# An attention probability split by one affine select on GpSimd instead of two products, the low weight halves of wo all on GpSimd, and a difference of values on VectorE

## The chip, the cores and the metric
The kernel runs on one core of one Trainium2 chip. The metric is device time in microseconds of one launch. Before the change the median of three runs is 810.45 us (809.56 to 811.89).

## The reference, cut to what matters
Three blocks work on x (4 sequences of 256 tokens, 512 channels): a feed-forward block with a router and low-rank experts, attention, and the feed-forward block again. The change lies in the attention, which has 32 query heads in 8 groups of 4 (one key/value head each) and a sliding window of 128:

```python
q = _rope((x @ wq).reshape(B, S, 32, 128), pos)
k = _rope((x @ wk).reshape(B, S, 8, 128), pos)
v = (x @ wv).reshape(B, S, 8, 128)
allowed = (j <= i) & (j > i - 128)
attn = softmax(where(allowed, q @ k.T * sm_scale, neg))
out = (attn @ v).reshape(B, S, 4096) @ wo
```

All is float32. A query of the second 128 tokens of a sequence sees keys of the first block with j > i - 128 and keys of the second block with j <= i. Within 128 columns these two sets don't overlap and fill the row, so one 128 x 128 tile P holds all its probabilities: column c stands for key c of block 1 where c <= row, and for key c of block 0 elsewhere.

## The kernel before, in words
Every float32 product is made of three passes in a shorter format: each operand is split in a high half (a rounded copy, made by ScalarE) and a low half (operand minus high half, made by VectorE or GpSimd), and TensorE computes high x high, high x low and low x high.

The attention runs over 8 groups g (the first and the last are written out, the six between are a loop), each with two halves hf (two sequences each, 512 tokens), each with 8 slots s. A slot is one head of one sequence; u counts all 128. TensorE's queue in a slot is, in this order: in slot 0 first the transposes of the values (`v_transpose`), then 9 of the 72 matmuls that project the next half's k, q0 to q3 and v (`project`, L1106), the scores of the next head (L1125 to L1128), the two transposes of the previous head's probabilities (`p_transpose`, L1136), and, for four heads at once, `values` (L1149, in slots 1 and 5) and `out_project` (L1165, in slots 2, 3, 6, 7). An `m` names the six projected tiles, 0 for k, 1 to 4 for q, 5 for v. Tiles 0 to 5 end in slots 1, 2, 3, 5, 6 and 7 of a half. They alternate between two PSUM banks A[0] and A[1]; the first matmul of a tile waits (`a_free`) until the tile two before has been read by `rope_cos`, or, for v, by `v_lo`.

Rope of a tile: ScalarE swaps its halves (`rope_swap`, L528), GpSimd multiplies them by the sine (`rope_sin`, L370), VectorE multiplies by the cosine (`rope_cos`, L782) and adds (`rope_sum`, L791), ScalarE makes the high half (L536), GpSimd the low half (`rope_lo`, L387).

Softmax of a head: VectorE adds masks and takes minima (`softmax_min`, L804 to L812; L812 merges the two key blocks of the second queries in one 128 x 128 tile), ScalarE exponentiates (L554), VectorE takes the reciprocal of the sum and multiplies twice (`softmax_norm`, L817 and L820), TensorE transposes, ScalarE copies the high half (`p_hi`, L562), VectorE makes the low half (`p_lo`, L826). Then GpSimd parts the tile of the second queries (`p_part`, L377): it waits for `p_lo` and multiplies both halves by a table with ones where the column is causal (to block 2 of pT) and by the complement (in place, block 1). `values` computes, for the second queries, block 1 x v0 + block 2 x v1, and waits (`parted`) ahead of these six matmuls.

Order on VectorE in a slot: `v_lo` in slot 0, an addition of the attention's output to x (L839), `softmax_norm`, in slot 5 of half 0 `wo_split`, `rope_sum`, `rope_cos`, `p_lo`, `softmax_min` of the next head, `o_lo` (L832) in slots 1 and 5. On GpSimd: `rope_sin`, `p_part`, `rope_lo`, `weights`.

Weights come by DMA in pieces of 128 x 512 through a ring of five buffers (`raw`); ScalarE makes the high halves (L500), and SyncE's queue starts the next piece when the low half of the one before in the same buffer is done. The low halves of wk, wq and wv are made on GpSimd (`split_lo`, L362). Of wo's four pieces the first two are made there in slot 4 of half 0, the other two on VectorE (`wo_split`, L861) in slot 5. The second pass of `out_project`, in slot 6, waits for all four.

Of the kernel before, what the change touches and what calls it, by code (L numbers as in the profile page):

```python
# [24 lines left out]
P = 128  # L25
# [50 lines left out]
def macaron(nc, x_in, wq, wk, wv, wo, w_base, b_base, w_router, lora_a, lora_b, ident_in, mask_in, side_in, rope_in, out):  # L76
    ctx = ExitStack()
    with ctx:
# [11 lines left out]
        side = sb("side", [P, 2, P])  # L90
# [96 lines left out]
        conv_hi, conv_lo, wo_lo = sem("w_hi_done"), sem("w_lo_done"), sem("wo_lo_done")  # L187
        a_done, a_free = sem("proj_done"), sem("proj_bank_read")
        vcopy_done, vt_done = sem("vT_copied"), sem("v_transposed")
# [5 lines left out]
        parted = sem("pT_parted")  # L195
# [8 lines left out]


# [14 lines left out]
        WO_POOL = G // 2  # L220

        def wk_lo(g):
            return 8 * g + 1

        def wq_lo(g, i):
            return 8 * g + 2 + i

        def wv_lo(g):
            return 8 * g + 6

        def wo_lo_pool(g, i):
            return 8 * g + 7 + i

        def wo_lo_dve(g, i):
            return 2 * g + 1 + i - WO_POOL

# [20 lines left out]
        def _(sp):  # L257
# [8 lines left out]
            sp.dma_start(side[:, :, :], side_in).then_inc(tables_landed, 16)  # L266
# [13 lines left out]
            def group(g, last):  # L280
                order = [("o", i) for i in range(G)]
                if not last:
                    order += [("k", 0)] + [("q", i) for i in range(KT)] + [("v", 0)]
                for kind, i in order:
                    if kind == "k":
                        sp.wait_ge(conv_lo, wv_lo(g))
                        off, src = 4, wk_src(wk, g + 1)
                    elif kind == "o":
                        sp.wait_ge(conv_lo, wq_lo(g, i))
                        off, src = i, wo[bass.ds(g * (G * DH) + i * DH, DH), :]  # L290
                    elif kind == "q":
                        if i < WO_POOL:
                            sp.wait_ge(conv_lo, wo_lo_pool(g, i))
                        else:
                            sp.wait_ge(wo_lo, wo_lo_dve(g, i))
# [34 lines left out]
        def _(pool):  # L330
            nc.gpsimd.memset(ones, 1.0).then_inc(preset, 1)
            nc.gpsimd.memset(ebuf[:, :, :, :], -1.0).then_inc(preset, 1)
            nc.gpsimd.memset(two[:, :, :], -1.0).then_inc(preset, 1)

# [37 lines left out]
            def p_part(u, s):  # L372

                pool.wait_ge(ptlo_done, u + 1)
                both, h = pT_both[:, :, 1, s % G, :], s % G
                for blk in (2, 1):
                    last = nc.gpsimd.tensor_tensor(pT_both[:, :, blk, h, :], both.bitcast(F32),  # L377
                                                   side[:, blk - 1, :].unsqueeze(1).broadcast_to([P, 2, P]), ALU.mult)
                last.then_inc(parted, 1)
# [9 lines left out]
            def weights(g, hf, s, last):  # L389
                if hf == 0 and s == 4:  # L390
                    for i in range(WO_POOL):
                        split_lo(wo_pos(g, i), (6 + i) % RING, wo_s[0][:, i, :], wo_s[1][:, i, :])
# [48 lines left out]
        def _(act):  # L441
# [96 lines left out]
            def v_copy(j):  # L538

                act.wait_ge(a_done, 6 * j + 6)  # L540
                act.wait_ge(sum_done, 5 * j + 4)
                nc.scalar.activation(swap[:, 1, :], A[1][:, :], ACT.Copy).then_inc(vcopy_done, 1)
# [119 lines left out]
        def _(dve):  # L662
# [130 lines left out]

            def v_lo(j, par):
                dve.wait_ge(vhi_done, j + 1)
                nc.vector.tensor_tensor(v[1][:, par, :, :], A[1][:, :].rearrange("p (t n) -> p t n", t=HT),
                                        v[0][:, par, :, :].bitcast(F32), ALU.subtract).then_inc(a_free, 1)
# [59 lines left out]
            def wo_split(g):  # L857

                for i in range(WO_POOL, G):
                    dve.wait_ge(conv_hi, wo_pos(g, i) + 1)  # L860
                    nc.vector.tensor_tensor(wo_s[1][:, i, :], raw[:, (6 + i) % RING, :], wo_s[0][:, i, :].bitcast(F32),  # L861
                                            ALU.subtract).then_inc(wo_lo, 1)

            def group(g, first, last):
                for hf in range(2):
                    for s in range(SLOTS):
# [10 lines left out]
                        if hf == 0 and s == 5:  # L877
                            wo_split(g)
# [4 lines left out]
                        if not (start and s == 0):  # L883
                            p_lo(u - 1, s - 1)
                        if s == 0 and last and hf == 1:
# [62 lines left out]
            dve.wait_ge(tables_landed, 48)  # L948
# [20 lines left out]
            rope_sum(0, 4)  # L969
            softmax_min(0, 0)  # L970
# [35 lines left out]
        def _(pe):  # L1006
# [104 lines left out]
            def v_transpose(j):  # L1111

                pe.wait_ge(vcopy_done, j + 1)
# [25 lines left out]
            def values(beta, par, b, j):  # L1139
# [4 lines left out]
                for i, blocks in enumerate((((0, 0),), ((1, 0), (2, 1)))):  # L1144
                    if i:
                        pe.wait_ge(parted, 4 * beta + 4)
                    todo = [(blk, kb, a, c) for blk, kb in blocks for a, c in PASSES]
                    for n, (blk, kb, a, c) in enumerate(todo):
                        last = mm(O[i][:, :], v[a][:, par, 2 * b + kb, :], pT[c][:, blk, :, :],  # L1149
# [3 lines left out]
            def out_project(beta, par, i, g):  # L1153
# [4 lines left out]
                for n, (a, c) in enumerate(((0, 0), (0, 1), (1, 0))):  # L1158
                    if c:
                        pe.wait_ge(conv_lo, wo_lo_pool(g, WO_POOL - 1))  # L1160
                        pe.wait_ge(wo_lo, wo_lo_dve(g, G - 1))
# [146 lines left out]
```

## Time and profile before
| | |
|---|---|
| median of 3 runs | 810.45 us |
| profiled execution, span from first to last instruction | 807.1 us |
| TensorE matmul busy | 739.6 us, 92% |
| VectorE busy | 677.0 us, 84% |
| GpSimd busy | 508.7 us, 63% |
| ScalarE busy | 417.0 us, 52% |
| granted TensorE clock, mean | 0.979 |

An engine's busy time in this profile holds the time in which one of its instructions has started and can't go on, so an instruction's duration can be longer than its work. PE is TensorE, DVE VectorE, ACT ScalarE, POOL GpSimd.

### The profile page before, as it was taken

How to read it: one execution, taken by the hardware profiler on the slowest of the kernel's cores; microseconds unless marked ns; L12 is line 12 of the kernel's file. 1: busy time of each engine (PE TensorE's matmuls, PEld its weight loads, DVE VectorE, ACT ScalarE, POOL GpSimd, SP SyncE). 2: the span in 40 equal slices, each digit the busy share in tenths (PEclk: the TensorE clock that was granted, in tenths of full speed). 3: DMA queues.
4: the chain of work that ended last, by engine and by line, in shares of the span. 5: the costliest groups of instructions: out<-in, count | busy, mean ns of one | idle time of the engine just before them, and what ended most of it. 6: DMA issues, size and time to landing. Idle time of an engine off the chain costs nothing.

```text
span 807.1 us, 14015 instructions
## 1 busy us (share of the span) xinstructions
PE 739.6 (92%) x3692; PEld 611.2 (76%) x3692; DVE 677.0 (84%) x2060; ACT 417.0 (52%) x1122; POOL 508.7 (63%) x578
## 2 busy tenths in 40 slices
PE   5989778999899989998999899999899899988998
PEld 3878557878777878787878777877788787876876
DVE  3888878988898888889888888888978898888795
ACT  2324474556655665555555555565557545654321
POOL 0384387766777667757775776577667776664720
PEclk8899999999999999999999999999999999999999
DMA  9040002100120011001100120002100210020002
GB/s 293 1 170 14 1 4 84 45 1 2 66 66 1 0 65 52 13 0 65 52 13 0 52 65 13 0 20 71 39 0 0 70 47 0 2 105 0 2 27 79
DMA packets 25986, 32.25 MB, mean 40 GB/s; under 512 B 5849, under 2 KB 14425, under 8 KB 25442
## 3 DMA queue, kind: packets, MB, share of 16 engines
q1 hardware_dynamic: 21216, 30.56, 11.5%
q10 hardware_dynamic: 4738, 1.31, 0.7%
q8 instruction: 14, 0.23, 0.1%
q14 instruction: 18, 0.15, 0.1%
HBM read 27.67 MB, written 4.19 MB: 39 GB/s over the span
## 4 chain that ended last, share of the span: by engine, by line
PE 51%; DVE 28%; issue 11%; ACT 5%; ACTq 2%; POOL 2%; DVEq 1%
PE bank L1106 17%; PE bank L1165 16%; DVE sm L812 4%; PE bank L1128 4%; PE bank L1149 4%; PE bank L1072 4%; DVE rot L791 3%; ACT prob L554 3%; DVE rot L782 2%; DVE wo_lo L861 2%; PE bank L1136 2%; DVE sm L805 2%; DVE prob L820 2%; DVE pT_hi_lo L826 2%; DVE oT_lo L832 2%
## 5 line engine op out<-in xcount | busy, mean ns | idle before, releaser
L377 POOL TENSOR_TENSOR pT_hi_lo<-pT_hi_lo,side 128x256 fp32r<-128x256 f32 x256 | 186.9, 751 | 118.6 <-DVE pT_hi_lo L826 118.6
L554 ACT ACTIVATE prob<-sm,nmax 128x128 f32<-128x128 f32 x256 | 101.0, 395 | 204.9 <-DVE sm L812 204.9
L370 POOL TENSOR_TENSOR swap<-swap,rope 128x512 f32<-128x512 f32 x80 | 105.8, 1322 | 95.5 <-ACT swap L528 95.5
L820 DVE TENSOR_SCALAR prob<-prob,rinv 128x128 f32<-128x128 f32 x256 | 123.9, 525 | 4.5
L528 ACT ACTIVATE swap<-bank 64x512 f32<-64x512 f32 x160 | 94.9, 593 | 11.3 <-PE bank L1106 8.7
L387 POOL TENSOR_TENSOR q_lo<-rot,q_hi 128x512 fp32r<-128x512 f32 x64 | 84.5, 1321 | 6.8 <-ACT q_hi L536 6.8
L1165 PE MATMUL bank<-wo_hi,oT_hi 128*128 128x512 f32 x256 | 79.4, 434 | 0.3 <-DVE x L839 0.3
L812 DVE TENSOR_TENSOR sm<-sm 128x128 f32<-128x128 f32 x128 | 79.3, 619 | 0.0
L1106 PE MATMUL bank<-xnT_hi,wq_hi 128*128 128x512 f32 x256 | 72.3, 395 | 6.5 <-DVE rot L782 5.3
L1106 PE MATMUL bank<-xnT_lo,wq_hi 128*128 128x512 f32 x256 | 73.4, 390 | 0.0
L1106 PE MATMUL bank<-xnT_hi,wq_lo 128*128 128x512 f32 x256 | 72.6, 396 | 0.9 <-POOL wq_lo L362 0.9
L562 ACT ACTIVATE pT_hi_lo<-bank 128x256 fp32r<-128x256 f32 x128 | 48.9, 382 | 46.4 <-PE bank L1136 38.3
L1165 PE MATMUL bank<-wo_lo,oT_hi 128*128 128x512 f32 x256 | 70.1, 396 | 0.0
L1165 PE MATMUL bank<-wo_hi,oT_lo 128*128 128x512 f32 x256 | 68.7, 390 | 0.0
L1149 PE MATMUL bank<-pT_hi_lo,v_hi 128*128 128x512 f32 x192 | 63.6, 412 | 1.7 <-POOL pT_hi_lo L377 0.9
L791 DVE TENSOR_TENSOR rot<-rot,swap 128x512 f32<-128x512 f32 x80 | 64.2, 803 | 0.0
L1106 PEld LDWEIGHTS bank<-xnT_hi,wq_hi 128*128 128x128 f32 x256 | 47.3, 188 | 20.0 <-DVE rot L782 8.7
L782 DVE TENSOR_TENSOR rot<-bank,rope 128x512 f32<-128x512 f32 x80 | 54.7, 684 | 9.0 <-ACT swap L528 9.0
L1136 PE MATMUL bank<-ident,prob 128*128 128x128 f32 x256 | 50.7, 281 | 10.7 <-DVE pT_hi_lo L826 10.7
L826 DVE TENSOR_TENSOR pT_hi_lo<-bank,pT_hi_lo 128x256 fp32r<-128x256 f32 x128 | 53.3, 416 | 8.2 <-ACT pT_hi_lo L562 6.9
L536 ACT ACTIVATE q_hi<-rot 128x512 fp32r<-128x512 f32 x64 | 40.2, 629 | 37.3 <-DVE rot L791 37.2
L1128 PE MATMUL bank<-k_hi_lo,q_hi 128*128 128x256 f32 x256 | 59.2, 314 | 0.0
(148 smaller groups left out, 1705.6 us busy)
## 6 DMA issues: line engine op xcount, KB each, us to landing
raw<-in_L_attn_wq SPq DMA_DIRECT2D x32, 256.0 KB, 2.9
raw<-in_L_attn_wo SPq DMA_DIRECT2D x32, 256.0 KB, 2.7
x<-in_L_attn_x SPq DMA_DIRECT2D x4, 512.0 KB, 7.8
raw<-in_L_attn_wk SPq DMA_DIRECT2D x8, 256.0 KB, 2.5
raw<-in_L_attn_wv SPq DMA_DIRECT2D x8, 256.0 KB, 2.6
out<-x SPq DMA_DIRECT2D x8, 256.0 KB, 2.0
raw<-in_L_ffn_W_base ACTq DMA_DIRECT2D x4, 256.0 KB, 5.3
wb_keep_hi<-q_hi SPq DMA_DIRECT2D x1, 1024.0 KB, 4.8
```

The lines of the kernel that those rows point to most:

```text
L370: nc.gpsimd.tensor_tensor(w, w, tab, ALU.mult).then_inc(t2_done, 1)
L377: last = nc.gpsimd.tensor_tensor(pT_both[:, :, blk, h, :], both.bitcast(F32), side[:, blk - 1, :].unsqueeze(1).broadcast_to([P, 2, P]), AL ...
L387: nc.gpsimd.tensor_tensor(lo, rot[:, m % 2, :], hi.bitcast(F32), ALU.subtract).then_inc(qlo_done, 1)
L528: last = nc.scalar.activation(swap[a:a + half, m % 2, :], A[m % 2][b:b + half, :], ACT.Copy)
L554: last = nc.scalar.activation(prob[:, s % 2, lo:hi], sm[:, s % 2, lo:hi], ACT.Exp, bias=nmax[:, s % 2, i:i + 1], scale=-1.0, accum_out=rsu ...
L791: nc.vector.tensor_tensor(rot[:, m % 2, :], rot[:, m % 2, :], swap[:, m % 2, :], ALU.add).then_inc(sum_done, 1)
L812: nc.vector.tensor_tensor(sm[:, s % 2, P:2 * P], sm[:, s % 2, P:2 * P], sm[:, s % 2, 2 * P:3 * P], ALU.min).then_inc(min_done, 1)
L820: last = nc.vector.tensor_scalar(prob[:, s % 2, lo:hi], prob[:, s % 2, lo:hi], rinv[:, s % 2, i:i + 1], None, ALU.mult)
L1106: last = mm(A[m % 2][:, :], w, xnT[b][:, d, hf * HALF:(hf + 1) * HALF], start=(i == 0), stop=(i == 11))
L1128: last = mm(S[s % 2][:, 2 * P:4 * P], q[a][:, hf, h, q1], k[c][:, hf, b * SEQ:(b + 1) * SEQ], start=(n == 0), stop=(n == 2))
L1149: last = mm(O[i][:, :], v[a][:, par, 2 * b + kb, :], pT[c][:, blk, :, :], start=(n == 0), stop=(n == len(todo) - 1))
L1165: last = mm(C[:, :], oT[a][:, par, i, h, :], wo_s[c][:, h, :], start=(h == 0 and n == 0), stop=(h == G - 1 and n == 2))
```

## The change
The values of the second key block are replaced by the difference v1 - v0: ScalarE copies only v0 of the transposed values to SBUF (two of the four 128-column blocks of A[1]), and a new VectorE instruction per half, `v_diff`, subtracts that copy from v1; `v_transpose` waits for it. Block 1 of pT then stays the whole P and is not written by `p_part`; block 2 is P where causal, zero elsewhere, by one affine select, so that P v0 + causal(P)(v1 - v0) equals the sum before. The number of matmuls stays. The wait for `parted` moves three matmuls later. The table `side` and its DMA go. All four low halves of wo are made on GpSimd in slot 4 of half 0, `wo_split` goes, and SyncE's waits follow.

```diff
             def p_part(u, s):
                 pool.wait_ge(ptlo_done, u + 1)
-                both, h = pT_both[:, :, 1, s % G, :], s % G
-                for blk in (2, 1):
-                    last = nc.gpsimd.tensor_tensor(pT_both[:, :, blk, h, :], both.bitcast(F32),
-                                                   side[:, blk - 1, :].unsqueeze(1).broadcast_to([P, 2, P]), ALU.mult)
-                last.then_inc(parted, 1)
+                pool.sem_inc(mask_turn, 1)
+                h = s % G
+                nc.gpsimd.affine_select(pT_both[:, :, 2, h, :], pT_both[:, :, 1, h, :].bitcast(F32),
+                                        pattern=[[0, 2], [1, P]], compare_op=ALU.is_ge, fill=zero,
+                                        base=0, channel_multiplier=-1).then_inc(parted, 1)
...
             def weights(g, hf, s, last):
                 if hf == 0 and s == 4:
-                    for i in range(WO_POOL):
+                    for i in range(G):
                         split_lo(wo_pos(g, i), (6 + i) % RING, wo_s[0][:, i, :], wo_s[1][:, i, :])
...
-                nc.scalar.activation(swap[:, 1, :], A[1][:, :], ACT.Copy).then_inc(vcopy_done, 1)
+                nc.scalar.activation(v_half(swap[:, 1, :], 0), v_half(A[1][:, :], 0), ACT.Copy).then_inc(vcopy_done, 1)
...
+            def v_diff(j):
+                dve.wait_ge(vcopy_done, j + 1)
+                nc.vector.tensor_tensor(v_half(swap[:, 1, :], 1), v_half(A[1][:, :], 1), v_half(swap[:, 1, :], 0),
+                                        ALU.subtract).then_inc(vdiff_done, 1)
...
-                        if hf == 0 and s == 5:
-                            wo_split(g)
...
                             p_lo(u - 1, s - 1)
+                        if m == 5:
+                            v_diff(2 * g + hf + 1)
...
-                    if i:
-                        pe.wait_ge(parted, 4 * beta + 4)
                     todo = [(blk, kb, a, c) for blk, kb in blocks for a, c in PASSES]
                     for n, (blk, kb, a, c) in enumerate(todo):
+                        if n == len(PASSES):
+                            pe.wait_ge(parted, 4 * beta + 4)
```

## Rows read from the trace of the kernel before

**Rows 1.** The page: busy time, share, instructions; then shares of the last-ended chain.
```profile
PE 739.6 (92%) x3692; PEld 611.2 (76%) x3692; DVE 677.0 (84%) x2060; ACT 417.0 (52%) x1122; POOL 508.7 (63%) x578
...
PE 51%; DVE 28%; issue 11%; ACT 5%; ACTq 2%; POOL 2%; DVEq 1%
```
**Rows 2.** TensorE's waits: total us, times, longest us.
```profile
PE bank L1106 <- DVE rot L782: 30.1, 17, 3.7
PE bank L1136 <- DVE pT_hi_lo L826: 10.7, 12, 1.7
```
**Rows 3.** Groups: busy us, mean ns of one, idle before and its releaser.
```profile
L1106 PE MATMUL bank<-xnT_hi,wv_hi 128*128 128x512 f32 x64 | 23.1, 448 | 25.2 <-DVE rot L782 24.8
```
**Rows 4.** Stretches: length, busy PE, PEld, DVE, ACT, POOL, PEclk, DMA share, GB/s.
```profile
388.57:473.17 84.60, 79.88 (x397) 66.48 (x396) 72.46 (x216) 48.88 (x133) 58.91 (x61) 0.98 0.10 31
...
125.00:128.40 3.40, 3.40 (x13) 2.96 (x12) 3.37 (x11) 2.27 (x7) 2.33 (x4) 0.50 0.16 57
208.60:212.00 3.40, 3.40 (x18) 2.95 (x19) 3.32 (x12) 1.44 (x5) 2.74 (x3) 1.00 0.41 146
...
715.50:718.90 3.40, 3.40 (x13) 2.97 (x12) 3.32 (x12) 2.15 (x7) 1.04 (x3) 0.50 0.22 39
```
**Rows 5.** Timeline of VectorE from 452.8 us: start, length, instruction, count.
```profile
452.83 0.42 DVE L826 TENSOR_TENSOR pT_hi_lo<-bank,pT_hi_lo 128x256 fp32r<-128x256 f32 x1 [0.52 <-ACT pT_hi_lo L562]
...
454.05 0.87 DVE L812 TENSOR_TENSOR sm<-sm 128x128 f32<-128x128 f32 x1
455.87 0.17 DVE L817 RECIPROCAL rinv<-rsum 128x2 f32<-128x2 f32 x1 [0.95 <-ACT prob L554]
456.07 2.58 DVE L820 TENSOR_SCALAR prob<-prob,rinv 128x128 f32<-128x128 f32 x2
458.57 2.37 DVE L861 TENSOR_TENSOR wo_lo<-raw,wo_hi 128x512 fp32r<-128x512 f32 x2
460.87 0.68 DVE L782 TENSOR_TENSOR rot<-bank,rope 128x512 f32<-128x512 f32 x1
```
**Rows 6.** Timeline of GpSimd over the same stretch.
```profile
453.34 1.43 POOL L377 TENSOR_TENSOR pT_hi_lo<-pT_hi_lo,side 128x256 fp32r<-128x256 f32 x2 [1.90 <-DVE pT_hi_lo L826]
454.73 1.33 POOL L387 TENSOR_TENSOR q_lo<-rot,q_hi 128x512 fp32r<-128x512 f32 x1
456.01 2.56 POOL L362 TENSOR_TENSOR wo_lo<-raw,wo_hi 128x512 fp32r<-128x512 f32 x2
458.51 1.28 POOL L370 TENSOR_TENSOR swap<-swap,rope 128x512 f32<-128x512 f32 x1
```
**Rows 7.** Timeline of TensorE: the stall of slot 5/6 and what follows it.
```profile
457.59 1.07 PE L1106 MATMUL bank<-xnT_hi,wq_lo 128*128 128x512 f32 x4
461.60 0.96 PE L1106 MATMUL bank<-xnT_hi,wv_hi 128*128 128x512 f32 x3 [2.94 <-DVE rot L782]
```
**Rows 8.** Lines L812 and L820: ns min/median/max of one, first and last start.
```profile
L812 DVE TENSOR_TENSOR sm<-sm x128: 285/856/1381, 94.1 to 755.7; 128x128 f32<-128x128 f32 x128
...
L820 DVE TENSOR_SCALAR prob<-prob,rinv x256: 272/286/1339, 97.7 to 757.6; 128x128 f32<-128x128 f32 x128
```
**Rows 9.** Groups: the removed, moved and nearest operations.
```profile
L377 POOL TENSOR_TENSOR pT_hi_lo<-pT_hi_lo,side 128x256 fp32r<-128x256 f32 x256 | 186.9, 751 | 118.6 <-DVE pT_hi_lo L826 118.6
L362 POOL TENSOR_TENSOR wo_lo<-raw,wo_hi 128x512 fp32r<-128x512 f32 x16 | 20.3, 1293 | 0.0
L826 DVE TENSOR_TENSOR pT_hi_lo<-bank,pT_hi_lo 128x256 fp32r<-128x256 f32 x128 | 53.3, 416 | 8.2 <-ACT pT_hi_lo L562 6.9
L249 POOL TENSOR_TENSOR nt<-nt,var 128x2 f32<-128x2 f32 x12 | 2.5, 205 | 0.9
```
**Rows 10.** Timeline of GpSimd at the start: its cheapest instruction of such width.
```profile
0.88 0.14 POOL L332 MEMSET ebuf<- 128x64 f32 x1
```
**Rows 11.** Timelines around a transpose of values: VectorE's low half, then TensorE.
```profile
428.41 0.41 DVE L826 TENSOR_TENSOR pT_hi_lo<-bank,pT_hi_lo 128x256 fp32r<-128x256 f32 x1
...
429.98 0.60 PE L1115 MATMUL bank<-ident,swap 128*128 128x128 f32 x4
```
**Rows 12.** Timeline of VectorE in slot 1 of half 1, behind two wq pieces.
```profile
480.33 2.57 DVE L820 TENSOR_SCALAR prob<-prob,rinv 128x128 f32<-128x128 f32 x2
```

More of the change, by code:

```diff
@@ L89, in macaron @@
         mask = sb("mask", [P, 3 * P])
-        side = sb("side", [P, 2, P])
         rope = sb("rope", [P, 4, SEQ])
@@ L186, in macaron @@
         raw_landed = [sem(f"raw_landed{i}") for i in range(RING)]
-        conv_hi, conv_lo, wo_lo = sem("w_hi_done"), sem("w_lo_done"), sem("wo_lo_done")
+        conv_hi, conv_lo = sem("w_hi_done"), sem("w_lo_done")
         a_done, a_free = sem("proj_done"), sem("proj_bank_read")
-        vcopy_done, vt_done = sem("vT_copied"), sem("v_transposed")
+        vcopy_done, vdiff_done, vt_done = sem("vT_copied"), sem("vT_diff"), sem("v_transposed")
         swap_done, t2_done, sum_done = sem("swap_done"), sem("sin_done"), sem("rope_sum_done")
@@ L194, in macaron @@
         rinv_done, norm_done = sem("rinv_done"), sem("norm_done")
-        parted = sem("pT_parted")
+        parted, mask_turn = sem("pT_parted"), sem("mask_turn")
         t_done, pthi_done, ptlo_done = sem("pT_done"), sem("pT_hi"), sem("pT_lo")
@@ L203, in wait, with v_half @@
                 eng.wait_ge(s, n)
+        def v_half(t, i):
+            return t.rearrange("p (b i n) -> p b i n", b=2, i=2)[:, :, i, :]
         def wk_pos(g):
@@ L216, in wo_pos, with wo_lo @@
             return 10 * g + 6 + i
-        WO_POOL = G // 2
         def wk_lo(g):
-            return 8 * g + 1
+            return 10 * g + 1
         def wq_lo(g, i):
-            return 8 * g + 2 + i
+            return 10 * g + 2 + i
         def wv_lo(g):
[L229 to L235, printed above, removed]
+            return 10 * g + 6
+        def wo_lo(g, i):
+            return 10 * g + 7 + i
         def rstd_steps(engine, then, t0, t1):
@@ L265, in _ @@
             sp.dma_start(mask[:, :], mask_in).then_inc(tables_landed, 16)
-            sp.dma_start(side[:, :, :], side_in).then_inc(tables_landed, 16)
             sp.dma_start(rope[:, :, :], rope_in).then_inc(tables_landed, 16)
@@ L291, in group @@
                     elif kind == "q":
[L292 to L295, printed above, removed]
+                        sp.wait_ge(conv_lo, wo_lo(g, i))
                         off, src = 5 + i, wq_src(g + 1, i)
@@ L333, in _ @@
             nc.gpsimd.memset(two[:, :, :], -1.0).then_inc(preset, 1)
+            zero = nc.gpsimd.to_reg(0.0)
             def bias(f, t):
@@ L855, in ffn_start @@
                     x_lo(2, 1)
[L857 to L862, printed above, removed]
             def group(g, first, last):
@@ L946, in _ @@
             ffn_out(0, NT // 2 - 1)
-            dve.wait_ge(tables_landed, 48)
+            dve.wait_ge(tables_landed, 32)
             rope_cos(0, 0)
@@ L969, in _ @@
             rope_sum(0, 4)
+            v_diff(0)
             softmax_min(0, 0)
@@ L1111, in v_transpose @@
             def v_transpose(j):
-                pe.wait_ge(vcopy_done, j + 1)
+                pe.wait_ge(vdiff_done, j + 1)
                 for t in range(HT):
@@ L1159, in out_project @@
                     if c:
-                        pe.wait_ge(conv_lo, wo_lo_pool(g, WO_POOL - 1))
-                        pe.wait_ge(wo_lo, wo_lo_dve(g, G - 1))
+                        pe.wait_ge(conv_lo, wo_lo(g, G - 1))
                     if a:
```

## The prediction
> **What bounds the kernel now.** I read the page first. TensorE is busy 92% of the span, and the chain that ended last is 51% TensorE and 28% VectorE [rows 1]: neither engine bounds it alone, so the question is where TensorE stands still and for whom. The list of waits answers: 30.1 us for the cosine product of rope (L782) and 10.7 us for the low half of the probabilities (L826), both VectorE's [rows 2]. Of the 30.1, the grouped lines give 24.8 to one place, the first matmul of a v tile [rows 3], once in each of 8 groups, 3.1 us each. Next the clock: a group takes 84.6 us at a mean of 0.98 [rows 4]. Right behind this stall the granted clock is 0.50, the lower level of 1.2 GHz, over 3.4 us in six of the eight groups, the first and last of which are shown, and 1.00 (2.4 GHz) behind the one of 208.6 and behind one more [rows 4]. At half clock 3.4 us hold 1.7 us of work, so the stall is followed by another 6 x 1.7 = 10 us of loss.
>
> Then I asked why VectorE is late there. L820 is 0.29 us in the median and up to 1.34; L812 is 0.29 at the least and 0.86 in the median [rows 8]. The long ones lie beside GpSimd. In one place two L820 take 2.58 us from 456.07 to 458.65 while GpSimd runs the two wo pieces from 456.01 to 458.57; the two of `wo_split` then take 2.37 with `rope_sin` beside them [rows 5, 6]. So a VectorE instruction with all its operands in SBUF waits until the running GpSimd instruction ends, gets in between two of them, and meets the next. L782 and L826, which read PSUM, don't wait. L812 shows the commonest case: `p_lo` ends at 453.25, GpSimd's first product starts at 453.34 and its second some 0.71 later; L812 starts at 454.05, 0.80 behind `p_lo` and just behind the start of the second product, and is held until that ends, 0.58 us lost [rows 5, 6]. More than half of the 128 heads show it, by the median.
>
> **Part 1, wo.** VectorE loses two L861 between L820 and the cosine product, 2.37 us [rows 5]. GpSimd gains two L362, 2 x 1.29 = 2.6 us, in slot 4 [rows 9]. I walk through the stall: with all else as before, L820 still ends at 458.65, held by the first two wo pieces; the cosine product starts there instead of at 460.87, and TensorE, free from 458.66, goes on about 0.6 us later instead of 2.94 [rows 5, 7]. That is 2.3 us per group. GpSimd's pieces three and four end at about 461.2, `rope_sin` of this slot at 462.5. They now hold L812 of slot 5 (near 460.4, to 461.2) and one of slot 6's two L820 under the wk piece, but all that stands over 1 us ahead of its old time. The second pass of `out_project` needs the fourth piece: TensorE is there near 461.9. SyncE's next wq pieces start with the same pieces at nearly the same time and have slot 6 to land.
>
> **Part 2, the select.** 256 products of 0.751 us go, 128 selects come [rows 9]. The trace has no select. From below: no input at all, a memset of 64 columns, is 0.14 us [rows 10]. From above: as slow as the two products, 1.50; nothing excludes more (a rival). I take the nearest row, one product of the same 128 x 256: 0.75 us. Then GpSimd is free, or at a boundary, at 0.09 + 0.05 (the added semaphore instruction, an estimate of mine) + 0.75 = 0.89 behind `p_lo`, L812 arrives at 0.80 and is held 0.1 instead of 0.6. Everything queued behind the product, `rope_lo` and the weight pieces, starts 0.65 earlier, and so L820 is held less: behind the two wq pieces it is 2.57 for two [rows 12]. With wo's part, L820 of slot 5 meets two wo pieces 0.6 us earlier, so that the cosine product ends near 458.7, when TensorE arrives: the stall goes but for 0.5 on average, 2.6 x 8 = 21 us. The clock had no stall of 3 us to fall after: 10 us. The other waits on VectorE, 30.1 - 24.8 + 10.7 = 16.0 [rows 2, 3], lie in half 1 at the end of a VectorE chain of four or five slots; saving about 0.5 per L812 and 0.6 at the L820s there is near 2 us per group, as much as the stalls. Some will be taken by what is late next, TensorE's wait for its own order or ScalarE's copy (8.2 us of idle at L826 already [rows 9]); I take 9 of the 16.
>
> The Trainium skill has a rule that would change this term. By it (GPSIMD Engine Reference, section 7, Performance pitfalls for Q7 kernels) a loop body that compares and selects runs at 1.03 to 2.03 cycles per element; with 256 elements at the 1.2 GHz of section 1 that is an estimate of 0.22 to 0.43 us of loop. No run here shows it; the products' 0.751 is the nearest that the trace has. By the rule the select would end before L812 arrives, which is the first rival below.
>
> **Part 3, v_diff.** 16 new VectorE instructions of 128 x 256 from PSUM: 0.416 by L826 [rows 9], 0.33 apart. They read PSUM and one SBUF tile like L826, so GpSimd doesn't hold them. ScalarE's copy halves in width. `p_lo` of slot 7 ends at 428.82; the difference ends near 429.2, and TensorE transposes at 429.98 [rows 11]: hidden by `out_project`, 0.8 us to spare; without that cover it would be 0.4 x 16 = 6.6. It does push `softmax_min` and so L812 and ScalarE's exponential back 0.33, 16 times, 5.3 us at most, and at least nothing, where TensorE is the later of the two. With the longer holds that wo's pieces make in slots 5 and 6 I charge 5 us in all. Ahead of the first group nothing covers VectorE's wait for ScalarE's copy: 1 us.
>
> **Part 4, the rest.** The wait for `parted` moved behind three matmuls and the table's DMA at the start cost nothing and gain under 1 us: TensorE's wait there is hidden in the 16.
>
> **Sum** against the profiled execution: 807.1 - 21 - 10 - 9 + 5 + 1 = 773.1 us. The run around it is 810.45 - 807.1 = 3.35 more (the median against this one execution): **776 us**. For this case alone, 764 to 788.
>
> **Rivals.**
> 1. *The select is fast, below 0.65 us.* Then the next GpSimd instruction (1.29 to 1.33 us, [rows 6, 9]) starts before L812 and holds it to 0.14 + D + 1.29, at D = 0.5 to 1.93 behind `p_lo`, against 1.52 now: 0.4 later wherever something is queued. L820 then finds GpSimd free more often. For it: a small two-input product costs 0.205, so the fixed part is small [rows 9]. Against: two-input products cost 0.751, and the select has to form its condition for each element. Price: the 9 us of part 2 are not gained and the stall of slot 5 keeps 0.2 more: 776 + 9 + 2 = 787.
> 2. *The select is as slow as both products, 1.2 to 1.6.* Only part 1 is left: 2.3 x 8 = 18, the clock's 10, less 5 + 1: 810.45 - 22 = 788.
> 3. *The select is slower than 1.7, and VectorE is held by it at L812 in nearly every slot.* L812 then waits D - 0.66 instead of 0.58, and all GpSimd work behind it is later. The gain of 22 us over some 110 heads is 0.2 each, so it decides from D = 1.5 + 0.2 = 1.7. At D = 2.0 it is 0.5 x 110 = 55 us: 810 + 55 - 22 = 843, slower. For it: no row bounds the select from above. Against: it reads one tensor, not two, and each product takes 0.75.
> 4. *The burst of four wo pieces moves the stall instead of taking it away*: L812 and L820 of slots 5 and 6 held by up to 2.6 us, as GpSimd works in its own order, and the next wait stands at slot 6 or 7. Gain of the v tile's stall halved and the clock's kept to half: 810 - 10 - 5 - 9 + 6 = 792.
>
> **How the numbers follow.** Forecast 48%, rival 1 16%, rival 2 11%, rival 3 12%, rival 4 13%. The predicted time is 776. The low end of the range is the forecast's own with all 16 us and no new cost, 810.45 - 21 - 10 - 16 = 763, taken down to 760; the high end takes in rivals 1, 2 and 4 with a few us, 805. Rival 3 is outside. Within 0.3% of 810.45 (808 to 813, about what a measurement can tell from no change) lie the seams between rivals 2, 4 and 3: 4%. Faster 84%, slower 12%.
>
> **What would show it.** The select's mean duration, 0.75, decides most: under 0.65 rival 1, over 1.7 rival 3. L812's median falls from 0.86 to about 0.4. The idle before the v tile's first matmul falls from 25.2 us to about 4, and no stretch at 0.50 follows it. A group takes near 80 us. L1115 doesn't wait for the new difference. GpSimd's busy time falls by 187 - 96 - 21 = 70 us. I am wrong if VectorE's chain still ends later than TensorE's queue in slot 5 though `wo_split` is gone.

## The result and the profile after

The changed kernel takes 777.57 us (median of 4 runs, 777.01 to 778.18) against 810.51 before: ratio 0.9591, 95% interval 0.9577 to 0.9606, so 33 us or 4.1% faster. The prediction was 776 with 760 to 805, and 84% on faster. Time and direction came out; several of the terms that make up the 776 did not, and their errors cancelled. That is what the experiments are about. The ratios below are to runs of the kernel before taken beside each kernel, whose medians lie from 809.9 to 811.2 us.

The page of the kernel after, against [rows 1]: busy times, then the shares of the chain that ended last.

```profile
PE 731.0 (94%) x3692; PEld 606.8 (78%) x3692; DVE 643.7 (83%) x2060; ACT 411.2 (53%) x1122; POOL 392.9 (51%) x466
...
PE 47%; DVE 31%; issue 10%; ACT 9%; ACTq 2%; DVEq 1%; POOL 0%
```

GpSimd lost 116 us of work, VectorE 33, and yet VectorE's share of the chain rose from 28% to 31%. TensorE's waits, as in [rows 2], and the one place of [rows 3]:

```profile
PE bank L1101 <- DVE rot L777: 13.3, 13, 2.2
...
PE bank L1131 <- DVE pT_hi_lo L827: 4.8, 4, 2.2
PE bank L1159 <- DVE x L840: 4.6, 8, 0.7
```
```profile
L1101 PE MATMUL bank<-xnT_hi,wv_hi 128*128 128x512 f32 x64 | 22.4, 436 | 12.1 <-DVE rot L777 12.1
```

The stall at the v tile fell from 25.2 to 12.1 us, the transposes' from 10.7 to 4.8; a new one of 4.6 stands at `out_project`, for the addition to x that frees its bank. The stretches, columns as in [rows 4]: one group, the 3.4 us behind the first v stall, and behind a later one.

```profile
375.90:456.30 80.40, 78.26 (x398) 65.37 (x397) 68.17 (x217) 48.17 (x133) 44.51 (x47) 1.00 0.11 33
124.20:127.60 3.40, 3.40 (x13) 2.91 (x13) 3.32 (x13) 1.74 (x6) 3.10 (x4) 0.50 0.51 165
446.00:449.40 3.40, 3.40 (x19) 2.89 (x19) 3.32 (x12) 1.96 (x6) 2.91 (x3) 1.00 0.51 151
```

A group takes 80.4 us in place of 84.6. Between 95 and 735 us the clock stood at its lower level twice for 3.4 us, before six times, and TensorE's gaps sum to 25.2 us where they were 44.5.

What such a stretch costs can be read inside one trace, because some groups have one and others, behind the same stall, have none. Here is a group of each kind in the kernel before (from one transpose to the same one of the next group), then in e2, the kernel after without its wo edit, where a stall of 2.5 us is left:

```profile
187.82:271.89 84.07, 78.80 (x399) 65.08 (x398) 72.36 (x217) 48.85 (x134) 58.90 (x61) 1.00 0.10 32
356.27:440.84 84.57, 79.85 (x398) 66.58 (x397) 72.44 (x217) 48.86 (x134) 58.91 (x61) 0.98 0.09 31
```
```profile
349.59:431.41 81.82, 79.27 (x398) 66.54 (x397) 69.62 (x219) 48.06 (x134) 41.88 (x44) 0.98 0.10 32
431.41:513.28 81.87, 78.22 (x399) 65.36 (x397) 69.63 (x219) 48.06 (x134) 41.89 (x44) 1.00 0.11 32
```

With the stretch TensorE is busy 1.05 us longer. Yet the group takes only 0.3 to 0.5 us longer before (84.4 to 84.6 against 84.1) and no longer in e2: at least half of it falls in time in which TensorE would have waited. Between groups without such a stretch the change is worth 84.1 - 80.4 = 3.7 us, 8 times, some 30 of the 33 us.

The new select and the two VectorE operations beside GpSimd, grouped (mean ns of one is the second number behind the bar), against [rows 9] and, for the next two, one line's minimum, median and maximum against [rows 8]:

```profile
L372 POOL TENSOR_SCALAR_AFFINE_SELECT pT_hi_lo<-pT_hi_lo 128x256 fp32r<-128x256 f32 x128 | 52.8, 413 | 145.8 <-DVE pT_hi_lo L827 145.0
```
```profile
L813 DVE TENSOR_TENSOR sm<-sm x128: 285/1185/1301, 96.0 to 725.6; 128x128 f32<-128x128 f32 x128
```
```profile
L821 DVE TENSOR_SCALAR prob<-prob,rinv x256: 272/285/1343, 98.5 to 727.3; 128x128 f32<-128x128 f32 x128
```

The select is 0.41 us, not 0.75. L813, the merge that was L812, did not get shorter: its median rose from 0.86 to 1.19. The timelines show why, first VectorE, then GpSimd, in slot 4:

```profile
438.69 0.42 DVE L827 TENSOR_TENSOR pT_hi_lo<-bank,pT_hi_lo 128x256 fp32r<-128x256 f32 x1
...
439.90 1.20 DVE L813 TENSOR_TENSOR sm<-sm 128x128 f32<-128x128 f32 x1
442.06 0.17 DVE L818 RECIPROCAL rinv<-rsum 128x2 f32<-128x2 f32 x1 [0.95 <-ACT prob L549]
442.26 2.57 DVE L821 TENSOR_SCALAR prob<-prob,rinv 128x128 f32<-128x128 f32 x2
444.75 0.68 DVE L777 TENSOR_TENSOR rot<-bank,rope 128x512 f32<-128x512 f32 x1
```
```profile
439.28 0.41 POOL L372 TENSOR_SCALAR_AFFINE_SELECT pT_hi_lo<-pT_hi_lo 128x256 fp32r<-128x256 f32 x1 [3.00 <-DVE pT_hi_lo L827]
439.66 1.30 POOL L382 TENSOR_TENSOR q_lo<-rot,q_hi 128x512 fp32r<-128x512 f32 x1
440.91 5.07 POOL L357 TENSOR_TENSOR wo_lo<-raw,wo_hi 128x512 fp32r<-128x512 f32 x4
445.92 1.30 POOL L365 TENSOR_TENSOR swap<-swap,rope 128x512 f32<-128x512 f32 x1
```

The select is over at 439.69, the low half of rope starts at 439.66, and L813, at 439.90, is held by that until 441.0. Two L821 still take 2.57 us beside the first two of the four wo pieces, and the cosine product L777 starts at 444.75 directly behind them; before, `wo_split` stood between.

**A measure for the holds.** For each kernel I took the VectorE instructions behind 95 us whose operands all lie in SBUF (the merge of the minima, the two products of the normalization, the rope sum, `wo_split`) and summed by how much each record is longer than a free one (0.288, 0.286, 0.684, 0.680), shorter ones counted as nothing. Before it is 119.8 us (merge 41, normalization 62, rope sum 8, wo 9), after 92.5 (75, 17, 0, none). This sum, TensorE's gaps and the count of stretches at half clock, the last two between 95 and 735 us, stand beside each run below. Ahead of 95 us, where the kernels do the same, the clock was at half for 10.2 to 17.1 us in one profiled execution and another, so a few us between two executions need not be the change's.

| kernel | median us | ratio to before, interval | holds us | gaps us | half clock |
|---|---|---|---|---|---|
| before | 810.5 | 1 | 119.8 | 44.5 | 6 |
| after | 777.6 | 0.9591, 0.9577 to 0.9606 | 92.5 | 25.2 | 2 |
| e1 wo's part only | 803.8 | 0.991, 0.9891 to 0.9928 | 126.1 | 43.0 | 1 |
| e2 select's part only | 789.6 | 0.975, 0.9726 to 0.9775 | 93.9 | 32.5 | 5 |
| e3 one product | 782.8 | 0.9659, 0.9635 to 0.9683 | 84.2 | 27.2 | 4 |
| e4 low half first | 768.9 | 0.9483, 0.9466 to 0.9499 | 73.8 | 22.8 | 3 |
| e5 yield | 761.7 | 0.9416, 0.9376 to 0.9457 | 59.2 | 20.3 | 0 |
| e6 one select for four | 781.2 | 0.9641, 0.9616 to 0.9666 | 87.3 | 26.6 | 5 |
| e7 no difference | 778.4 | 0.9601, 0.9583 to 0.9619 | 98.5 | 28.9 | 0 |
| e8 e4, wk later | 753.3 | 0.9288, 0.9270 to 0.9306 | 63.9 | 13.8 | 0 |
| e9 e5, wk later | 767.7 | 0.9472, 0.9449 to 0.9494 | 66.5 | 23.4 | 0 |
| e11 e3, yield | 767.8 | 0.9477, 0.9454 to 0.9500 | 63.5 | 22.2 | 0 |
| e12 e1, wk later | 810.2 | 1.0003, 0.9991 to 1.0015 | 133.9 | 44.8 | 3 |
| e13 products, order of e8 | 814.4 | 1.0053, 1.0036 to 1.0071 | 130.9 | 45.5 | 3 |

### The profile page after: what moved, and what is told of

Its sections match the earlier page's. It is cut to its first block, busy times and chain, and to the rows that moved or that the text cites. A ratio compares the mean times of both kernels' runs of the same rounds, so it can differ in the third digit from the quotient of the medians.

```text
span 776.5 us, 13949 instructions
## 1 busy us (share of the span) xinstructions
PE 731.0 (94%) x3692; PEld 606.8 (78%) x3692; DVE 643.7 (83%) x2060; ACT 411.2 (53%) x1122; POOL 392.9 (51%) x466
## 4 chain that ended last, share of the span: by engine, by line
PE 47%; DVE 31%; issue 10%; ACT 9%; ACTq 2%; DVEq 1%; POOL 0%
PE bank L1101 16%; PE bank L1159 12%; DVE sm L813 7%; PE bank L1144 5%; PE bank L1067 4%; ACT prob L549 4%; PE bank L1123 3%; DVE sm L806 3%; DVE rot L777 3%; DVE oT_lo L833 2%; DVE rot L786 2%; DVE pT_hi_lo L827 2%; DVE sm L805 2%; PE bank L1131 2%; ACTq L442 2%
## 5 line engine op out<-in xcount | busy, mean ns | idle before, releaser
L372 POOL TENSOR_SCALAR_AFFINE_SELECT pT_hi_lo<-pT_hi_lo 128x256 fp32r<-128x256 f32 x128 | 52.8, 413 | 145.8 <-DVE pT_hi_lo L827 145.0
L813 DVE TENSOR_TENSOR sm<-sm 128x128 f32<-128x128 f32 x128 | 112.1, 876 | 0.0
L382 POOL TENSOR_TENSOR q_lo<-rot,q_hi 128x512 fp32r<-128x512 f32 x64 | 82.6, 1291 | 7.6 <-ACT q_hi L531 7.6
L821 DVE TENSOR_SCALAR prob<-prob,rinv 128x128 f32<-128x128 f32 x256 | 78.9, 350 | 4.5
L1159 PE MATMUL bank<-wo_hi,oT_hi 128*128 128x512 f32 x256 | 75.1, 415 | 5.0 <-DVE x L840 4.6
L777 DVE TENSOR_TENSOR rot<-bank,rope 128x512 f32<-128x512 f32 x80 | 54.9, 687 | 12.9 <-ACT swap L523 12.9
L818 DVE RECIPROCAL rinv<-rsum 128x2 f32<-128x2 f32 x128 | 20.6, 161 | 47.0 <-ACT prob L549 47.0
L827 DVE TENSOR_TENSOR pT_hi_lo<-bank,pT_hi_lo 128x256 fp32r<-128x256 f32 x128 | 53.4, 417 | 6.2 <-ACT pT_hi_lo L557 5.9
L786 DVE TENSOR_TENSOR rot<-rot,swap 128x512 f32<-128x512 f32 x80 | 57.2, 716 | 0.0
L1159 PEld LDWEIGHTS bank<-wo_lo,oT_hi 128*128 128x128 f32 x256 | 48.1, 188 | 10.8
```

Source lines behind the costliest of these rows:

```text
L382: nc.gpsimd.tensor_tensor(lo, rot[:, m % 2, :], hi.bitcast(F32), ALU.subtract).then_inc(qlo_done, 1)
L777: nc.vector.tensor_tensor(rot[:, m % 2, :].rearrange("p (b s) -> p b s", b=2), A[m % 2][:, :].rearrange("p (b s) -> p b s", b=2), rope[:, ...
L786: nc.vector.tensor_tensor(rot[:, m % 2, :], rot[:, m % 2, :], swap[:, m % 2, :], ALU.add).then_inc(sum_done, 1)
L813: nc.vector.tensor_tensor(sm[:, s % 2, P:2 * P], sm[:, s % 2, P:2 * P], sm[:, s % 2, 2 * P:3 * P], ALU.min).then_inc(min_done, 1)
L821: last = nc.vector.tensor_scalar(prob[:, s % 2, lo:hi], prob[:, s % 2, lo:hi], rinv[:, s % 2, i:i + 1], None, ALU.mult)
L1159: last = mm(C[:, :], oT[a][:, par, i, h, :], wo_s[c][:, h, :], start=(h == 0 and n == 0), stop=(h == G - 1 and n == 2))
```

## The experiments

**The parts, each alone.** e1 is the kernel before with the wo edit, e2 the kernel after with it taken back:

```diff
-        WO_POOL = G // 2
+        WO_POOL = G                 # e1, on the kernel before; wo_split and its waits go
...
+                        if hf == 0 and s == 5:
+                            wo_split(g)    # e2, on the kernel after; pieces 0 and 1 stay on GpSimd
```

> The kernel before with all four low halves of wo on GpSimd and nothing else. Theory A (the parts add up, as the prediction has them: wo's part is worth the 2.3 us of the v tile's stall in each of 8 groups and the 10 us at half clock, less some 5): ratio 0.973, near 788 us, the idle before the v tile's first matmul from 25.2 to 5 to 12 us, no stretch of the attention at 0.50 after the first group. Theory B (nearly all of the 33 us is wo's): 777 to 781 us. Theory C (the longer burst of two-product parting and four pieces holds VectorE elsewhere): 800 us or more.

> The kernel after with the last two low halves of wo back on VectorE in slot 5: select, difference and moved wait alone. Theory A: the v tile's stall stays near 2.3 us in each group and the half clock follows it in some, so only the other waits are gained: 800 us. Theory B (nearly nothing is the select's, since L813 is held longer by what L821 is held less): 808 to 811 us.

Measured 803.8 and 789.6. The wo edit alone gives 7 us where the prediction had 22 (rival 2's sum), the rest alone 21. Together 33, so the wo edit is worth 12 on top of the rest. In e1 the v tile's stall did fall, from 25.2 to 7.0 us, to 0.64 in each group behind the first, where the prediction's walk had 0.6. But TensorE has other waits. First that tile's group, then the waits:

```profile
L1101 PE MATMUL bank<-xnT_hi,wv_hi 128*128 128x512 f32 x64 | 22.0, 429 | 7.0 <-DVE rot L779 6.5
```
```profile
PE bank L1101 <- DVE rot L779: 12.3, 17, 1.4
PE bank L1131 <- DVE pT_hi_lo L823: 12.1, 20, 1.7
PE bank L1159 <- DVE x L836: 11.0, 9, 1.8
```

The 11.0 at `out_project` is new: VectorE, relieved ahead of the cosine product, is held behind it (the rope sum's holds went from 8 to 17 us, the normalization's from 62 to 68), and the addition to x comes late in the next slots. This is rival 4 as the prediction described it, the stall moved on, and theory C on e1. Theory A, which is the prediction's sum, is 16 us off on e1 and 10 on e2, in opposite directions.

**One product in place of the select.** This builds the duration that I had forecast:

```diff
-                nc.gpsimd.affine_select(pT_both[:, :, 2, h, :], ...)
+                nc.gpsimd.tensor_tensor(pT_both[:, :, 2, h, :], pT_both[:, :, 1, h, :].bitcast(F32),
+                                        side[:, 1, :].unsqueeze(1).broadcast_to([P, 2, P]), ALU.mult)
```

> The kernel after with one product of P by the causal table (to block 2 alone) in place of the select: 0.75 us where the select takes 0.41, all else the same. Theory A (the holds go by the order of starts: L813 arrives 0.80 behind the end of p_lo and is held by whatever GpSimd has begun by then): the merge of minima L813 is held about 0.1 instead of 0.9, its median falls from 1.19 to 0.3 to 0.4 us although GpSimd works longer, and the time falls: 768 to 775 us. Theory B (the shorter GpSimd instruction is the better one, holds even out over L813 and L821): 779 us or more.

Measured 782.8, 5.2 above the kernel after. The merge went as theory A says, the time as theory B: grouped lines of e3, then of the kernel after,

```profile
L822 DVE TENSOR_SCALAR prob<-prob,rinv 128x128 f32<-128x128 f32 x256 | 118.6, 505 | 4.5
L814 DVE TENSOR_TENSOR sm<-sm 128x128 f32<-128x128 f32 x128 | 56.6, 442 | 0.0
```
```profile
L813 DVE TENSOR_TENSOR sm<-sm 128x128 f32<-128x128 f32 x128 | 112.1, 876 | 0.0
L821 DVE TENSOR_SCALAR prob<-prob,rinv 128x128 f32<-128x128 f32 x256 | 78.9, 350 | 4.5
```

so the merge is free (0.29 in the median), and the normalization takes up most of what it gave (merge from 75 to 20 us, normalization from 17 to 57, rope sum from 0 to 8). Matching the end of each held record with the GpSimd instruction that ended just before it tells by what: in the kernel after L821 is held by the wo pieces (16.6 us) and by next to nothing else, in e3 L822 by these (16.6), the sine product (14.6), the pieces of wq, wv and wk (22.0) and the product (3.3), and not once by the low half of rope. Why VectorE now meets them is open. The sum of holds is 8 us smaller, the time is not. The v tile's stall is all but gone (2.4 us), as the prediction had it for this duration (about 4); the waits at the transposes (10.0) and at `out_project` (9.1) stand in its place. Groups of e3 without a stretch at half clock, and with one:

```profile
340.08:420.88 80.80, 78.00 (x398) 65.24 (x397) 67.49 (x217) 48.49 (x132) 50.02 (x46) 1.00 0.11 32
501.80:583.22 81.42, 79.31 (x398) 66.54 (x397) 67.59 (x217) 48.47 (x132) 50.03 (x46) 0.98 0.10 32
```

The kernel after's take 80.4. So 0.4 to 0.5 us in each of 8 groups and 0.6 more in four make 6 us, about the 5.2 measured. The two gaps that come before such a fall, and the stretch behind them:

```profile
210.77 0.41 PE L1132 MATMUL bank<-ident,prob 128*128 128x128 f32 x2 [0.74 <-DVE pT_hi_lo L828]
212.44 1.46 PE L1160 MATMUL bank<-wo_hi,oT_hi 128*128 128x512 f32 x4 [1.27 <-DVE x L841]
```
```profile
213.10:216.50 3.40, 3.40 (x10) 2.62 (x9) 3.07 (x12) 2.64 (x7) 1.68 (x2) 0.50 0.01 2
```

Behind two gaps of 0.74 and 1.27 us with 0.41 us of work between, the clock fell in four groups of e3 as it did behind the single 2.9 us before; behind the same two gaps it stayed up in the other groups. The kernel after's single 1.32 (and 0.60 eight us later) was followed by no fall in any group. A second gap of that size is not needed, though: e6 has 0.19, then 1.42, and fell in four groups too, one of them here:

```profile
292.91 1.60 PE L1160 MATMUL bank<-wo_hi,oT_hi 128*128 128x512 f32 x4 [1.42 <-DVE x L841]
```
```profile
293.40:296.80 3.40, 3.40 (x9) 2.64 (x9) 2.94 (x12) 2.89 (x8) 1.55 (x2) 0.50 0.00 0
```

**The order on GpSimd.** e4 turns two lines of its queue, e8 also moves wk's piece from slot 5 to 6:

```diff
-                            p_part(...)          # then rope_lo
-                            rope_lo(...)
+                            rope_lo(...)         # e4: then p_part
+                            p_part(...)
...
-                if hf == 0 and s == 5 and not last:
+                if hf == 0 and s == 6 and not last:     # e8: wk's piece
```

> The kernel after with GpSimd's queue turned in a slot: the low half of rope (L382) ahead of the select. Theory A: it then runs before p_lo ends, the select ends 0.5 us behind p_lo, before L813 arrives; L813 at its free 0.29 in these five of eight slots, time 766 to 774 us. Theory B (the low half moves ahead and holds the two L821 or the rope sum instead, which costs the same): 776 to 780 us with L821's mean up from 0.35.

> The kernel with the low half of rope ahead of the select (768.9 us), and wk's low half moved from slot 5 to slot 6 of half 0. There the chain of stalls at slot 7 (0.43 at the transposes, 1.42 at out_project, for the addition to x) ends in L821 1.56 and L786 1.79 us, held by wk's piece and the sine product behind the four wo pieces. Theory A (the holds of slot 6 are what is late): both stalls shrink, 757 to 764 us. Theory B (the piece holds something else in slot 7 instead): 767 to 771 us.

Measured 768.9 and 753.3, the second below all its bounds (its profiled execution, 756.7, was the longest of five). e4's time is as theory A has it, its reason is not: the merge is not free. Here are `p_lo` and the merge in e4, and GpSimd's low half:

```profile
434.63 0.42 DVE L827 TENSOR_TENSOR pT_hi_lo<-bank,pT_hi_lo 128x256 fp32r<-128x256 f32 x1 [0.40 <-ACT pT_hi_lo L557]
...
435.85 0.80 DVE L813 TENSOR_TENSOR sm<-sm 128x128 f32<-128x128 f32 x1
```
```profile
435.20 1.30 POOL L382 TENSOR_TENSOR q_lo<-rot,q_hi 128x512 fp32r<-128x512 f32 x1 [2.94 <-ACT q_hi L531]
```

The low half waits for ScalarE's high half, which is ready only after `p_lo`, so it doesn't run before it; but it starts 0.15 behind `p_lo` and not 0.55, and the merge is held 0.5 instead of 0.9. The holds fall to 73.8 us, while the stall at `out_project` grew to 10.4 us. e8 takes that away too:

```profile
PE bank L1131 <- DVE pT_hi_lo L827: 5.7, 5, 1.8
...
PE bank L1159 <- DVE x L840: 2.1, 9, 0.3
```
```profile
366.97:444.25 77.28, 77.08 (x397) 65.40 (x396) 64.44 (x217) 48.33 (x134) 44.95 (x47) 1.00 0.12 34
```

A group takes 77.3 us with TensorE busy 77.1 of them: there TensorE's queue is the bound. This is the fastest version.

**Letting VectorE go first.** e5 keeps the order and makes what follows the select wait for the minima; e9 adds the move of wk's piece:

```diff
+                        if (split is not None and split < 5) or ((hf, s) in ((0, 4), (0, 5), (1, 0)) and not last):
+                            pool.wait_ge(min_done, 16 * g + 8 * hf + s + 2)
```

> The kernel after, where the low half of rope and the weight pieces that GpSimd has queued behind the select wait for the minima (L813 and its line) of the same slot: VectorE goes first at L813 in every slot with something queued, and nothing else changes. Theory A (the hold at L813, 0.9 us long in most heads, is on the path in the slots where VectorE is late): L813 falls from 112 us to under 50, L821 rises a little from 90, time 764 to 772 us. Theory B (holds only move: what GpSimd starts 0.9 later holds the next L821, as with the one product): L821 above 120 us and the time 776 to 784 us.

> The kernel after with both cures: what follows the select waits for the minima, and wk's piece stands in slot 6. The yielding run has 9.6 us of stalls at out_project left, of the kind that the wk piece made. Theory A (the same cure takes them): 751 to 756 us, as the run with the low half of rope first. Theory B (wk's piece, held back by the wait, comes late for slot 7): 758 us or more.

e5: 761.7, 16 us below the kernel after, for a wait added and nothing taken away. The merge and what waits for it now:

```profile
L815 DVE TENSOR_TENSOR sm<-sm x128: 285/288/839, 94.8 to 709.0; 128x128 f32<-128x128 f32 x128
...
  POOL q_lo L382: 39.2, 60
  POOL k_hi_lo L382: 8.6, 15
```

The merge's holds fell from 75 us to 3; those of the normalization rose from 17 to 39 and those of the rope sum from 0 to 17. So more than half of the 72 us moved and 33 went. That the place where GpSimd's instructions start costs time is so shown by a run that takes no work away; it delays them for all that follows too, and not the merge alone. Three of e5's four runs took 761.6 to 761.8 us and one 766.7. e9 missed: 767.7 (766.9 to 768.5), worse than e5. Its waits at `out_project`, which the move was to cure, are as e5's (9.5 and 9.6), and it has others,

```profile
PE bank L1103 <- POOL wq_lo L357: 2.8, 7, 0.4
...
PE bank L1112 <- DVE swap L794: 2.6, 8, 0.6
```

the transposes of the values now wait for the difference, eight times, and the last wq pieces come later than in e5 (1.7 us). A group takes 79.4 us, in e5 78.7. The time is theory B's; these waits explain part of it.

**One select for four heads.**

```diff
-                pool.wait_ge(ptlo_done, u + 1)        # each head
+                if s % G == G - 1:                    # each fourth
+                    pool.wait_ge(ptlo_done, u + 1)
+                    nc.gpsimd.affine_select(pT_both[:, :, 2, :, :], pT_both[:, :, 1, :, :].bitcast(F32),
+                                            pattern=[[0, 2], [0, G], [1, P]], ...)
```

> The kernel after with one select over four heads (128 x 1024) in place of four (128 x 256). From 0.19 fixed and 0.22 for 256 columns the one is about 1.1 us. Theory A (what counts is whether GpSimd starts something between the end of p_lo and L813): in three of four slots the low half of rope no longer waits for p_lo, L813 is free there, 766 to 774 us. Theory B (the select's total time counts): 128 x 0.41 = 53 us become 32 x 1.1 = 35 us, worth at most 2 us: 775 to 779 us.

Measured 781.2, beside both theories. The select's size is as expected, and GpSimd's low half of rope now waits for ScalarE alone:

```profile
L383 POOL TENSOR_TENSOR q_lo<-rot,q_hi 128x512 fp32r<-128x512 f32 x64 | 83.1, 1298 | 65.0 <-ACT q_hi L532 65.0
...
L373 POOL TENSOR_SCALAR_AFFINE_SELECT pT_hi_lo<-pT_hi_lo 128x1024 fp32r<-128x1024 f32 x32 | 35.0, 1094 | 111.8 <-DVE pT_hi_lo L828 111.8
```

The merge's holds fell to 42 us, the normalization's rose to 45, and the clock fell five times. Less GpSimd time in sum is no gain by itself. The long select also holds VectorE: the merge here starts 0.62 behind it and ends 0.14 after it, 0.61 in place of 0.29, as in 29 others:

```profile
240.44 0.61 DVE L814 TENSOR_TENSOR sm<-sm 128x128 f32<-128x128 f32 x1
```
```profile
239.82 1.09 POOL L373 TENSOR_SCALAR_AFFINE_SELECT pT_hi_lo<-pT_hi_lo 128x1024 fp32r<-128x1024 f32 x1 [2.91 <-DVE pT_hi_lo L828]
```

**Without the difference.**

```diff
-                nc.scalar.activation(v_half(swap[:, 1, :], 0), v_half(A[1][:, :], 0), ACT.Copy).then_inc(vcopy_done, 1)
+                nc.scalar.activation(swap[:, 1, :], A[1][:, :], ACT.Copy).then_inc(vcopy_done, 1)
...
-                        if m == 5:
-                            v_diff(2 * g + hf + 1)
...
-                pe.wait_ge(vdiff_done, j + 1)
+                pe.wait_ge(vcopy_done, j + 1)
```

> The kernel after without the difference: ScalarE copies both value blocks as before and the transposes wait for that, so block 2 of P is multiplied by v1 instead of v1 - v0 (left out: the difference, and with it the equality of the sum). Prediction's term: 0.33 us on VectorE 16 times, 5.3 us at most, of which I charged part of 5 us. Theory A (on the path in the half where VectorE is late): 773 to 776 us. Theory B (hidden behind TensorE's out_project): within 0.2% of the kernel after, 776 to 779 us.

Measured 778.4 against 777.6: hidden, theory B. The run also brings back ScalarE's wider copy (0.58 us in place of 0.36), so it prices the difference less what the narrower copy saves. In the kernel after L827 of slot 7 is followed by the difference and the transposes start behind `out_project` without a wait:

```profile
455.38 1.08 PE L1159 MATMUL bank<-wo_hi,oT_lo 128*128 128x512 f32 x4
456.29 0.60 PE L1110 MATMUL bank<-ident,swap 128*128 128x128 f32 x4
```

**Is it the order or the select?** e11 puts the yield on e3, e12 moves wk's piece in e1, and e13 gives the kernel before, with its two products, the whole order of e8 (wo on GpSimd, wk later, low half first); the edits are those above.

> The kernel with one product in place of the select (782.8 us), where what follows it on GpSimd waits for the minima as in the run where the kernel after yields (761.7 us). Both then free L813 of what follows; the select or product itself is over (0.14 + 0.75 = 0.89 behind p_lo) 0.1 after L813 arrives or before. Theory A (the duration under 0.8 us is worth nothing once the order is right): 760 to 765 us. Theory B (the shorter instruction brings everything behind it forward): 768 us or more.

> The kernel before with all wo pieces on GpSimd (803.8 us), and wk's piece moved from slot 5 to slot 6. That kernel lost the v tile's stall (24.3 to 5.9 us) but has new ones, 11.0 us at out_project for the addition to x and 12.1 at the transposes. Theory A (they are the burst's: four wo pieces, sine, two products and the wk piece in a row hold L820 and the rope sum of slot 6): they shrink as they did with the select, 790 to 797 us, which is what the prediction had for this part. Theory B (the two products hold L812 in every slot and that is the bound): 800 to 804 us.

> The kernel before with its two products, all wo pieces on GpSimd, wk's piece in slot 6 and the low half of rope ahead of the products: GpSimd's order of the fastest run so far (753.3 us with select and difference). Theory A (what the select is worth is its 1.02 us less of GpSimd time between p_lo and L813: 0.14 + 1.43 = 1.57 still holds L812 for 0.6 in each head): 775 to 785 us, so some 25 us are the select's in this order too. Theory B (the order was all): 755 to 762 us.

e11: 767.8, 15 below e3, 6 above e5, at the edge of theory B. With the yield the 0.34 us between product and select is so worth about 6 us by the medians; the intervals of e5 and e11 touch, and of the profiled executions a group takes 78.7 and 79.0. e12: 810.2, no gain over before and 6 lost on e1, outside both theories: the stall at `out_project` grew from 11.0 to 14.9, and why is open. e13: 814.4, slower than before (ratio above 1 by 0.36% at least) and 61 us above e8, which has the same order with the select. Both of my figures for it missed: the two products don't only hold the merge, TensorE now also waits for them at `values`,

```profile
PE bank L1144 <- POOL pT_hi_lo L374: 17.6, 23, 1.9
...
PE bank L1159 <- DVE x L836: 12.7, 16, 1.5
```

because the low half ahead of the products makes the parting late (it ends 2.9 us behind `p_lo` in the median, before 1.5), and all six matmuls of the second queries wait for it. With the kernel after only three do, three matmuls later. No run tells that algebra apart from the select's shortness: e3 and e11 have both the one product and the new algebra, and one product in e8's order, or the late wait with two products, was not run. How much of the 61 us is whose is so not shown.

## Why the prediction was right, and where it was not

**What bounds it** held: TensorE stands still for VectorE, and VectorE for GpSimd. e5 shows it: with no work taken away, an order in which VectorE goes first gives 16 us.

**Its own signs** mostly went against the forecast. The select took 0.41 us, below the 0.65 of rival 1; the merge's median rose to 1.19 where about 0.4 was forecast; the v tile's stall kept 12.1 us and not 4, and a stretch at half clock followed the first; GpSimd's busy time fell by 116 us and not 70. The stall that is left is what the prediction named as the sign of being wrong: in slot 5 VectorE's chain still ends later than TensorE's queue. Only the group's 80 us and the difference, for which TensorE waits 0.6 us in all, came as said. The total was right by luck.

**Part 2, the select's duration, failed.** I took the nearest row, 0.75 us; it is 0.413. From the two sizes measured, (1.094 - 0.413) / 768 columns is 0.887 ns each and 0.186 us fixed. The Trainium skill's rule that I set beside my choice (GPSIMD Engine Reference, section 7, 1.03 to 2.03 cycles per element for a compare and select) was the better guide: 0.887 ns at its 1.2 GHz is an estimated 1.06 cycles. The nearest row was one with two inputs, and I had in hand a fixed part of 0.2 that left all the doubt in the slope.

**Rival 1's mechanism came true and its price did not.** Below 0.65 us the next GpSimd instruction starts before the merge and holds it to 0.14 + D + 1.29. At D = 0.41 that is 1.84 behind `p_lo`; in the timelines above `p_lo` ends at 439.11 and the low half of rope at 440.96, 1.85 behind, with the merge's own end 0.14 later. L813 went from 79 to 112 us. But I priced it at 787 from the merge alone. The same instruction is over before the normalization starts, so that L821's holds fell from 62 to 17 us; the rival's own sentence said that L820 would be free more often, and its sum left it out. The forecast's mechanism, built as e3, costs 782.8, not 776: there the merge is free and the v tile's stall gone, as forecast, but the normalization is held 57 us in sum, where the prediction had it held less. The two cases lie in the other order than I had them.

**Part 1, wo, was mis-sized**: 22 us predicted, 7 measured alone (e1), 12 on top of the rest. The v tile's stall, 21 us by the prediction, lost 13 with the select and 18 in e1, and those 18 are what the walk of part 1 gives (2.3 x 8). What failed lies behind the walk, which ended at the cosine product: one slot on, the longer row of GpSimd instructions held the normalization and the rope sum (e1's holds 126, more than before), and TensorE stopped 11 us at `out_project`, 1 more at the transposes and 2 more for the wq pieces. I charged 5 us for all that together with the difference, of which nearly nothing is the difference's (e7). The rest of the miss is the clock's term.

**The other waits** of part 2: 9 us of 16 predicted. By waits, 16.0 became 13.3 - 12.1 + 4.8 = 6.0, with 4.6 new at `out_project`, so some 5 went; in e3, the duration that the 9 was worked out for, they grew to 22 (10.0 + 9.1 + 4.9 - 2.0). TensorE's waits at `values` for the parting, 1.7 us at most, went too. The whole part is 21 us alone and 26 on top of e1, where the prediction had 34 - 22 = 12.

**The clock** was priced too high: 10 us for six stretches, 1.7 each, as if all of the lost work lay on the path. Groups of the kernel before with and without one differ by 0.3 to 0.5 us, so the six were worth 2 to 3 us together. I also had it that a stall under 3 us costs no clock; e3 shows a fall behind two of 0.74 and 1.27, e6 behind 1.42, and the kernel after behind the first v tile's 2.25. That the stall at the v tile need not go away wholly for the clock to stay up was right.

**Part 3**: the difference is hidden, as said. **Sum**: wo's part, with the clock in it, was 10 to 15 us too good, the select's 9 to 14 too poor. A right total from wrong terms: the 33 us would not have told them apart, e1 to e3 did.

## What to carry to other kernels

Where VectorE's SBUF instructions wait out whole GpSimd instructions, don't price a GpSimd edit by its own length or by one instruction that it holds: go through all of VectorE's SBUF instructions in the slot, because a hold that leaves one is often met by the next. Nor is the sum of the holds the price (e3's is 8 us smaller than the kernel after's, its time 5 longer); what counts is a hold ahead of something that TensorE waits for. Arrange GpSimd's queue so that nothing long starts just ahead of them (a turned order was worth 9 us here and a wait for VectorE's result 16, the turned order with one piece moved 24), and try it again when the instructions change, as the same order made the kernel with two products slower. Don't price a stretch at half clock by the work that it loses: compare groups with and without one, here 0 to 1.5 us (none in e2, 1.5 in e4) where the lost work said 1.7. A stall taken from one place of a queue shared by three engines has to be followed for at least one more slot.

## What the runs showed of the hardware that I had not expected

An affine select on GpSimd of 128 x 256 float32 takes 0.413 us and one of 128 x 1024 1.094, 0.887 ns for each further column, where the instructions with two tensors take 2.1 (0.751 for a product of 256 columns and 1.293 for a difference of 512, [rows 9]). It has one SBUF input and holds VectorE's SBUF instructions like a product with two (e6, 0.61 for 0.29). And the granted clock fell to 0.50 for 3.4 us behind gaps of 0.74 and 1.27 us with 0.41 us of work between (e3), or of 0.19 and 1.42 (e6), in four groups each and not in the others; such a stretch made a group 0.3 to 0.5 us longer before, and no longer in e2.
